# Query rotation without a second projection: DVE reads one PSUM bank with its partition halves exchanged

## The chip, the cores and the metric

The kernel runs on one core of one Trainium2 chip. The metric is the device time of that core for one execution, in microseconds; the kernel before took 1685.34, 1689.40 and 1690.72 us in three runs, median 1689.4. PE is the matrix engine (TensorE), DVE the vector engine (VectorE), ACT the activation engine (ScalarE), POOL is GpSimd, SP the engine that issues DMAs.

## The reference, cut to what matters

The input is 16 sequences of 512 tokens with 128 channels. The program is two layers; each is half a feed-forward step, a mixing step, and another half feed-forward step. Only the first layer's opening stage is touched by the change: layer norm and feed-forward, then layer norm and the query, key and value projections with rotary embedding.

```
s = x @ Win + bin                                # 128 -> 64 channels
h = relu(s[..., None] * W1 + b1)                 # 16 hidden values per channel
x = x + 0.5 * ((h * W2).sum(-1) + b2) @ Wout ...
n = layernorm(x)
q = n @ Wq      # 16 heads of 8
k = n @ Wk      # 4 heads of 8
v = n @ Wv
q = q * cos + rotate_half(q) * sin               # rotate_half: (x1, x2) -> (-x2, x1)
k = k * cos + rotate_half(k) * sin
```

## The kernel before, in words

The stage is `mlp_layer(..., "qkv")`. It works on two sequences (W = 2, called b = 0 and 1) per turn, eight turns' worth of sequences, in a software pipeline: in one turn the code takes the statistics of the newest pair of sequences (`ahead`), transposes and projects the next (`head`), closes the feed-forward step of the one before (`middle`), and makes queries, keys and values of the last (`tail`). Three turns fill the pipeline, the fourth is the first with a `tail`, four turns run in a hardware loop (`Fori`), and three empty it. Each engine runs its own list of instructions in the order in which the code writes them; semaphores join them. All matmuls of this stage have fp32 operands, and each appears in the trace as two records.

The columns of Wq are laid out so that channel p and channel p + 64 (modulo 128) are the two that a rotation joins. Before, PE projects the queries twice: with `wq` (plain) and with `wqs` (columns swapped by half), into two PSUM banks `r_ps[2b]` and `r_ps[2b+1]`. DVE multiplies the first by the cosine table into `a`, the second by the signed sine table into `b` (`rope`, L675), POOL adds `a` and `b` (L614) and then splits the sum in three bf16 parts together with ACT (L547, L551, L620, L626); SP writes the parts to DRAM (L381, L388). Keys go the same way, with 16 channels for each of both sequences in one bank (64 rows used).

The order of the work around the change, on each engine, for one turn in which all four roles are filled:

- PE: 16 matmuls that contract the hidden values (`channels`, L429; for each hidden row j those of sequence 0 and then of sequence 1, each waiting for its `m_hid` tile), transposes for the tail (L282), the output projection (`output`, L442, after ACT has made `m_g_t`, L557), transposes for the head (L282), queries of sequence 0 (L455), the input projection (L487), queries of sequence 1 (L455), keys (L462), values (L469).
- DVE: statistics of the next pair, the residual addition (L686, when PE's L442 is done), statistics of the middle pair, then rotation of queries 0 (L675 twice), five hidden tiles of sequence 0 (`hidden`, L666), rotation of queries 1, five hidden tiles of sequence 1, rotation of the keys, copy of the values (L698).
- ACT: `m_g_t` (L557), copies of transposed tiles, `m_s` (L571, after L487), the other three hidden tiles of each sequence (L575), the normalisations (L219), the parts.
- POOL: L635, parts of the turn before, square roots (L192, L198), then the sums `a + b` (L614).

The query banks are reused in the same turn: keys go to banks 0 and 1 after DVE's reads of queries 0 (`rope_read`), values to bank 2 after DVE's first read of queries 1.

Of the kernel before, what the change touches and what calls it, by code (L numbers as in the profile page):

```python
# [9 lines left out]
ALU = mybir.AluOpType  # L10
# [3 lines left out]
P = 128  # L14
NB = 16
T = 512
D = 128
C = T // P
EPS = 1e-5

NH, NKV = 16, 4
HD = D // NH
# [7 lines left out]
HALF = P // 2  # L30
# [13 lines left out]
W = 2  # L44
# [3 lines left out]

PACK = [("ident", P), ("win2", P), ("bin2", 1), ("w1p", HT), ("b1p", HT), ("w2p", HT), ("b2p", 1), ("wout2", D), ("pairsum", P),
        ("mhalf", W * C), ("wu", M * 4), ("wtop", M), ("maskf", P), ("self", 2 * P), ("gw", E), ("rowbase", 1),  # L50
        ("wq", D), ("wqs", D), ("wk", NKV * HD), ("wks", NKV * HD), ("wv", NKV * HD), ("wo", D)]
PACK_LATE = [("cosq", T), ("sinq", T), ("iota", T)]


# [262 lines left out]
def mlp_layer(nc, sem, h, xres, tail_kind, name, x_in=None, loads=None, v_all=None,  # L317
# [7 lines left out]
    with ExitStack() as tmp:  # L325
# [5 lines left out]
        xhat2_t = [t(f"xhat2_t{b}", [P, T], F32) for b in range(W)]  # L331
# [6 lines left out]
        r_ps = [bank(f"r{j}") for j in range(4)]  # L338
# [30 lines left out]
        with nc.Block() as block:  # L369
# [50 lines left out]
            def _(pe):  # L420
# [13 lines left out]
                def output(i, tail):  # L434

                    pe.wait_ge(g_read, i + 1)
                    for b in range(W):
                        if qkv and tail is not None:

                            after(pe, rope_read, tail * 2 * NT)  # L440
                        for c in range(C):
                            mm = pe.matmul(y_ps[b][:, c * P:(c + 1) * P], g_t[:, c * P:(c + 1) * P], h["woutz"][:, b, :],  # L442
                                           start=True, stop=True)
                        mm.then_inc(y_full, 1)

                def queries(i, b):
                    for j, wt in enumerate(("wq", "wqs")):
                        if b == 1 and j == 0:

                            after(pe, v_read, i)  # L450
                        if b == 0 and j == 0:

                            after(pe, rope_read, i * 2 * NT)
                            pe.wait_ge(x_added, min((i + 2) * W, NB) if isinstance(i, int) else (i + 2) * W)
                        pe.matmul(r_ps[2 * b + j][:], h[wt][:], xhat2_t[b][:], start=True, stop=True).then_inc(rope_full, 1)  # L455

                def keys(i):

                    for j, wt in enumerate(("wk", "wks")):
                        pe.wait_ge(rope_read, i * 2 * NT + j + 1)  # L460
                        for b in range(W):
                            mm = pe.matmul(r_ps[j][b * KR:(b + 1) * KR, :], h[wt][:], xhat2_t[b][:], start=True, stop=True)  # L462
                        mm.then_inc(rope_full, 1)

                def values(i):
                    pe.wait_ge(rope_read, i * 2 * NT + 3)
                    for b in range(W):
                        for c in range(C):
                            mm = pe.matmul(r_ps[2][:, (b * C + c) * KR:(b * C + c + 1) * KR], xhat2_t[b][:, c * P:(c + 1) * P], h["wv"][:],  # L469
                                           start=True, stop=True)  # L470
                    mm.then_inc(v_full, 1)

# [182 lines left out]
            @block.vector  # L655
            def _(dve):
                v = nc.vector

                def hidden(i, *parts):
                    for j in range(made):  # L660
                        for b in parts:
                            dve.wait_ge(s_read, i * W + b + 1)

                            after(dve, hid_used, (i - 1) * HT + j + 1)

                            v.tensor_scalar(hid[b][j][:], s_in[b][:], h["w1p"][:, j:j + 1], h["nb1p"][:, j:j + 1],  # L666
                                            ALU.mult, ALU.max).then_inc(hid_done, 1)

                def rope(i, x):
                    n, rows = TILES[x]  # L670

                    after(dve, parts_out[x], i * OUT[x])
                    for j, (dst, tab) in enumerate((("a", "cos"), ("b", "sin"))):
                        dve.wait_ge(rope_full, (i * NT + x) * 2 + j + 1)
                        v.tensor_tensor(rot[n][dst][:], r_ps[(2 * x + j) % 4][0:rows, :], h[tab + n[0]][:], ALU.mult).then_inc(rope_read, 1)  # L675

                def turn(ahead, head, middle, tail):
                    if ahead is not None:
                        if x_in is not None:
                            dve.wait_ge(x_loaded, ahead + 1)  # L680
                        moments(dve, norm1, ahead)
                    if middle is not None:
                        dve.wait_ge(bias_added, middle + 1)
                        for b in range(W):
                            dve.wait_ge(y_full, middle * W + b + 1)
                            v.tensor_tensor(xres[:, middle * W + b, :], y_ps[b][:], xres[:, middle * W + b, :], ALU.add).then_inc(x_added, 1)  # L686
                        dve.wait_ge(x_added, middle * W + W)
                        moments(dve, norm2, middle)
                    if not qkv and head is not None:
                        hidden(head, *range(W))  # L690
                    for x in range(NT if qkv else 0):
                        if tail is not None:
                            rope(tail, x)
                        if head is not None and x < W:
                            hidden(head, x)
                    if qkv and tail is not None:
                        dve.wait_ge(v_full, tail + 1)
                        v.tensor_copy(v_all[:, bass.ds(tail * W, W), :],  # L698
                                      r_ps[2][:, 0:W * C * KR].rearrange("p (b x) -> p b x", b=W)).then_inc(v_read, 1)
                    if not qkv and tail is not None and not is_first(tail):  # L700
                        gate.keep(dve, tail - 1)
                    if not qkv and ahead is not None:
                        norm1.apply_dve(dve, ahead, xt_full)

                pipeline(dve, turn)
                if not qkv:
                    gate.keep(dve, TURNS - 1)
                    gate.softmax(dve)
# [943 lines left out]
def layouts(i):  # L1652
# [16 lines left out]
        "wq": wq.reshape(D, D), "wqs": wq[:, swap].reshape(D, D), "wk": wk.reshape(D, -1), "wks": wk[:, swap].reshape(D, -1),  # L1669
# [49 lines left out]
```

## Time and profile before

| | |
|---|---|
| three runs | 1685.34, 1689.40, 1690.72 us |
| profiled execution: own time / span | 1689.98 / 1688.3 us |
| stage of the change | from 0 to the first attention matmul at 225.31 us |
| PE busy, whole span | 1445.3 us (86%) |
| DVE / ACT / POOL busy | 1266.1 / 1161.0 / 776.1 us |
| mean granted TensorE clock | 0.925 |

In the rows below, times are microseconds from the span's start. A timeline row merges equal instructions that follow each other: start, length of the whole group, engine, line, operation, output and inputs, shape, count, and in brackets how long the engine was idle before it and what ended that. PE is the matmul, PEld its weight loads. A clock of 1.00 is 2.4 GHz, 0.50 is 1.2 GHz.

### The profile page before, as it was taken

To read this page: it belongs to the slowest core of one execution; us is meant where nothing else is said; L and a number is where in the kernel's file an instruction comes from. 1 tells how busy PE (TensorE), PEld (TensorE's weight loads), DVE (VectorE), ACT (ScalarE), POOL (GpSimd) and SP (SyncE) were. 2 spreads that over 40 slices of the span, in tenths; PEclk is the share of its full clock that TensorE was granted. 3 is DMA by queue.
4 is the path that set the end of the run, shared out by engine and by line. 5 is a ranking of instruction groups with operands and counts; after the bars stand their busy time and mean duration, and the time that the engine had idled before them with its cause. 6 is when DMAs were issued, how large, how long until landed. Compare 5 with 4: busy or idle time off the path is not lost. (4 is left out here: it accounts for less than half of the span.)

```text
span 1688.3 us, 40713 instructions
## 1 busy us (share of the span) xinstructions
PE 1445.3 (86%) x12722; PEld 1002.4 (59%) x12722; DVE 1266.1 (75%) x3158; ACT 1161.0 (69%) x2439; POOL 776.1 (46%) x1204
## 2 busy tenths in 40 slices
PE   3899859999999999969980899999968708999998
PEld 1455434545445454425550799999835508999997
DVE  3677568888888888737848577877788585778776
ACT  3788527777777777757862688778656507787875
POOL 2578734545454444424424666554022106665540
PEclk9999959999999999979985899999978758999999
DMA  5022211111111111000112111111001101111110
GB/s 153 10 70 84 88 31 41 45 39 46 41 44 46 39 44 41 10 1 26 37 38 100 37 38 38 33 30 26 1 13 44 44 0 40 51 51 50 48 36 25
DMA packets 84640, 70.92 MB, mean 42 GB/s; under 512 B 16752, under 2 KB 78000, under 8 KB 84528
## 3 DMA queue, kind: packets, MB, share of 16 engines
q1 hardware_dynamic: 76336, 52.62, 11.2%
q0 software_dynamic: 8192, 16.79, 3.9%
q8 instruction: 72, 1.18, 0.3%
q14 instruction: 40, 0.33, 0.1%
HBM read 46.81 MB, written 22.54 MB: 41 GB/s over the span
## 5 line engine op out<-in xcount | busy, mean ns | idle before, releaser
L1081 DVE TENSOR_REDUCE at_negmax<-at_s_ps 128x2 f32<-128x1024 f32 (+3 forms) x384 | 389.4, 1044 | 65.0 <-PE at_s_ps L858 57.6
L987 ACT ACTIVATE at_p<-at_x_ps 128x512 f32<-128x512 f32 x640 | 355.2, 596 | 97.3 <-PE at_x_ps L870 90.6
L1301 POOL DMA_INDIRECT e_x_in<-xn,e_row_c x256 | 258.9, 1011 | 145.8 <-issue 79.6
L1042 POOL TENSOR_SCALAR_AFFINE_SELECT at_p<-at_p 128x256 f32<-128x256 f32 (+1 forms) x448 | 190.4, 439 | 242.5 <-ACT at_p L987 242.4
L870 PE MATMUL at_x_ps<-qr,kr 50*128 50x512 bf16 (+3 forms) x1024 | 226.8, 304 | 18.7 <-ACT at_p L987 11.0
L1422 DVE TENSOR_TENSOR e_hid_lo<-e_hid,e_hid_hi 128x512 fp32r<-128x512 f32 x256 | 177.2, 692 | 83.0 <-ACT e_hid_hi L1386 70.3
L853 PE MATMUL at_s_ps<-kr,qr 48*128 48x512 bf16 (+3 forms) x1024 | 188.1, 311 | 19.2 <-PEq L1636 12.8
L1385 ACT ACTIVATE e_hid<-e_h_ps 128x512 f32<-128x512 f32 x256 | 154.8, 605 | 41.3 <-PE e_h_ps L1327 36.5
L886 PE MATMUL at_o_ps<-at_p,at_va 128*32 128x512 f32 (+3 forms) x2048 | 178.8, 445 | 0.0
L870 PEld LDWEIGHTS at_x_ps<-qr,kr 50*128 50x128 bf16 x1024 | 66.4, 94 | 153.0 <-ACT at_p L987 137.7
L1327 PE MATMUL e_h_ps<-e_x_hi,w_hi 128*128 128x256 f32 x512 | 156.7, 306 | 0.0
L858 PE MATMUL at_s_ps<-maskb,selb 64*128 64x64 bf16 x2048 | 156.3, 193 | 0.0
L1386 ACT ACTIVATE e_hid_hi<-e_h_ps 128x512 fp32r<-128x512 f32 x256 | 155.7, 608 | 0.0
L1327 PE MATMUL e_h_ps<-e_x_hi,w_lo 128*128 128x256 f32 x512 | 146.0, 285 | 0.0
L1327 PE MATMUL e_h_ps<-e_x_lo,w_hi 128*128 128x256 f32 x512 | 145.6, 284 | 0.0
L1337 PE MATMUL e_yt_ps<-e_hid_hi,w_lo 128*128 128x256 f32 x512 | 144.3, 282 | 0.0
L1337 PE MATMUL e_yt_ps<-e_hid_hi,w_hi 128*128 128x256 f32 x512 | 144.1, 281 | 0.0
L1337 PE MATMUL e_yt_ps<-e_hid_lo,w_hi 128*128 128x256 f32 x512 | 144.0, 281 | 0.0
L858 PEld LDWEIGHTS at_s_ps<-maskb,selb 64*128 64x128 bf16 x2048 | 124.7, 98 | 31.7 <-issue 3.4
L1378 ACT ACTIVATE e_x_hi<-e_t_ps 128x256 fp32r<-128x256 f32 x128 | 49.5, 386 | 135.5 <-PE e_t_ps L1316 124.3
L1355 PE MATMUL e_acc_ps<-e_hot,e_y_hi 128*128 128x512 f32 x256 | 111.6, 436 | 3.0 <-DVE e_hot L1441 3.0
L1441 DVE TENSOR_SCALAR e_hot<-pack_late,e_loc_c 128x512 fp32r<-128x512 f32 x256 | 114.1, 488 | 0.0
(196 smaller groups left out, 3391.2 us busy)
## 6 DMA issues: line engine op xcount, KB each, us to landing
qr<-q_parts SPq DMA_DIRECT2D x128, 48.0 KB
kr<-k_parts SPq DMA_DIRECT2D x128, 48.0 KB
xres<-in_x_dram SPq DMA_DIRECT2D x8, 512.0 KB, 7.4
qr<-q_parts SPq DMA_DIRECT2D x128, 32.0 KB
xn<-m_n_xhat SPq DMA_DIRECT2D x16, 256.0 KB
e_x_in<-xn,e_row_c POOLq DMA_INDIRECT x256
xn<-sc_n_xhat SPq DMA_DIRECT2D x16, 256.0 KB
out_dram<-xres SPq DMA_DIRECT2D x16, 256.0 KB
```

The source lines that it names most:

```text
L853: pe.matmul(s_ps[k % 2][:, half * T + a * w:half * T + (a + 1) * w], qr[u][rows, q0:q0 + P], kr[u][rows, g * T:g * T + w], start=True, sto ...
L858: mm = pe.matmul(s_ps[k % 2][:, at:at + HALF], h["selb"][rows, x * P:(x + 1) * P], h["maskb"][rows, x * HALF:(x + 1) * HALF], start=False, ...
L870: mm = pe.matmul(x_ps[i % 2][:, at:at + T - c * P], kr[u][rows, g * T + c * P:g * T + (c + 1) * P], qr[u][rows, q0 + c * P:q0 + T], start= ...
L886: mm = pe.matmul(o_ps[32 * j:32 * j + 32, c * P:T], va[u][:, c, g, :], p_sb[g % 2][:, i, at:at + T - c * P], start=(c == 0 and g % 2 == 0) ...
L987: a.activation(p_sb[g % 2][:, i, :], x_ps[i % 2][:], ACT.Exp, scale=SCALE).then_inc(x_read, 1)
L1042: sel = gp.affine_select(out=part, in_=part, compare_op=ALU.is_ge, fill=0.0, base=0, pattern=[[0, n] for n in part.shape[1:-1]] + [[1, P]] ...
L1081: v.tensor_reduce(out, scored, AX.X, ALU.max, negate=True).then_inc(s_read, 1)
L1301: nc.gpsimd.indirect_dma_start(out=x_in[k][u][:], out_offset=None, in_=xn_dram, in_offset=bass.IndirectOffsetOnAxis(ap=row_c[k][:, u:u + 1 ...
L1327: mm = pe.matmul(h_ps[half][:, f, :], w1[:, k, at:at + P], x[k % 2][:], start=(j == 0), stop=(j == len(pairs) - 1))
L1337: mm = pe.matmul(yt_ps[:], w2[:, k, f * D:(f + 1) * D], x[k % 2][:, f, :], start=(f == 0 and j == 0), stop=(f == FC - 1 and j == len(pairs ...
L1386: a.activation(hid_hi[k % 2][:, half * HC:(half + 1) * HC, :], h_ps[half][:], ACT.Gelu).then_inc(gelu_done, 1)
L1422: v.tensor_tensor(hid_lo[k % 2][:, chunks, :], hid[half][:], whole(hid_hi[k % 2][:, chunks, :]), ALU.subtract).then_inc(hl_done, 1)
```

## The change

The weights `wqs` are gone from the packed constants (128 columns less in the one DMA that loads them), and with them one of the two query matmuls of each sequence, 16 in all. DVE's cosine product is as before. The sine product becomes two instructions of 64 partitions each: the lower half of `b` from the upper half of the bank, the upper half of `b` from the lower half. `rope_read` still rises twice per query tile, the second time at the last of the three.

The banks are dealt out anew: queries 0 in bank 0, queries 1 in bank 2, keys in banks 1 and 3 (which no query uses now, so the wait ahead of the keys goes), values in bank 0 once DVE has read queries 0 whole. Two waits for `v_read` move with the values' bank.

```
-        ("wq", D), ("wqs", D), ("wk", NKV * HD), ...
+        ("wq", D), ("wk", NKV * HD), ...
 def queries(i, b):
-    for j, wt in enumerate(("wq", "wqs")):
-        if b == 1 and j == 0:
-            after(pe, v_read, i)
-        if b == 0 and j == 0:
-            after(pe, rope_read, i * 2 * NT)
-            pe.wait_ge(x_added, ...)
-        pe.matmul(r_ps[2 * b + j][:], h[wt][:], xhat2_t[b][:], ...).then_inc(rope_full, 1)
+    if b == 0:
+        after(pe, rope_read, i * 2 * NT)
+        after(pe, v_read, i)
+        pe.wait_ge(x_added, ...)
+    pe.matmul(r_ps[2 * b][:], h["wq"][:], xhat2_t[b][:], ...).then_inc(rope_full, 2)
 def keys(i):
-        pe.wait_ge(rope_read, i * 2 * NT + j + 1)
...
-            mm = pe.matmul(r_ps[j][b * KR:(b + 1) * KR, :], ...)
+            mm = pe.matmul(r_ps[2 * j + 1][b * KR:(b + 1) * KR, :], ...)
 def values(i):
-    pe.wait_ge(rope_read, i * 2 * NT + 3)
+    pe.wait_ge(rope_read, i * 2 * NT + 2)
...
 def rope(i, x):
-    for j, (dst, tab) in enumerate((("a", "cos"), ("b", "sin"))):
-        dve.wait_ge(rope_full, (i * NT + x) * 2 + j + 1)
-        v.tensor_tensor(rot[n][dst][:], r_ps[(2 * x + j) % 4][0:rows, :], h[tab + n[0]][:], ALU.mult).then_inc(rope_read, 1)
+    if x < W:
+        full = r_ps[2 * x]
+        dve.wait_ge(rope_full, (i * NT + x) * 2 + 2)
+        v.tensor_tensor(r["a"][:], full[:], h["cosq"][:], ALU.mult).then_inc(rope_read, 1)
+        v.tensor_tensor(r["b"][0:HALF, :], full[HALF:P, :], h["sinq"][0:HALF, :], ALU.mult)
+        v.tensor_tensor(r["b"][HALF:P, :], full[0:HALF, :], h["sinq"][HALF:P, :], ALU.mult).then_inc(rope_read, 1)
```

On PE, in the first turn that has a tail, the rows before are these: transposes, two matmuls of queries 0, two of the input projection, two of queries 1, four of keys, eight of values.

```order
L282 MATMUL m_xt_ps<-pack,m_n_xhat 128x128 x8
L455 MATMUL m_r_ps<-m_xhat_t,pack 128x512 x2
L487 MATMUL m_s_ps<-m_xhat_t,pack 128x512 x2
L455 MATMUL m_r_ps<-m_xhat_t,pack 128x512 x2
L462 MATMUL m_r_ps<-m_xhat_t,pack 32x512 x4
L469 MATMUL m_r_ps<-pack,m_xhat_t 128x32 x8
```

The same place on PE in the changed kernel, whose lines are numbered a little lower:

```order
L282 MATMUL m_xt_ps<-pack,m_n_xhat 128x128 x8
L453 MATMUL m_r_ps<-m_xhat_t,pack 128x512
L484 MATMUL m_s_ps<-m_xhat_t,pack 128x512 x2
L453 MATMUL m_r_ps<-m_xhat_t,pack 128x512
L459 MATMUL m_r_ps<-m_xhat_t,pack 32x512 x4
L466 MATMUL m_r_ps<-pack,m_xhat_t 128x32 x8
```

One matmul ahead of the input projection and one behind it are gone; nothing else has moved.

On DVE, the same turn before and after, from the rotation of queries 0 to the copy of the values:

```order
 L675 TENSOR_TENSOR m_q0a<-m_r_ps,pack_late 128x512
-L675 TENSOR_TENSOR m_q0b<-m_r_ps,pack_late 128x512
-L666 TENSOR_SCALAR m_hid<-m_s,pack,nb1p 128x512 x5
+L676 TENSOR_TENSOR m_q0b<-m_r_ps,pack_late 64x512
+L677 TENSOR_TENSOR m_q0b<-m_r_ps,pack_late 64x512
+L663 TENSOR_SCALAR m_hid<-m_s,pack,nb1p 128x512 x5
 L675 TENSOR_TENSOR m_q1a<-m_r_ps,pack_late 128x512
-L675 TENSOR_TENSOR m_q1b<-m_r_ps,pack_late 128x512
-L666 TENSOR_SCALAR m_hid<-m_s,pack,nb1p 128x512 x5
```

Each query tile has three products instead of two, and both stand ahead of the hidden tiles of sequence 1 (the second L666 group).

## Rows read from the trace of the kernel before

**Rows 1.** Busy time by stretch: PE, PEld, DVE, ACT, POOL, clock, DMA, GB/s.

```profile
103.00:124.00 21.00, 20.12 (x102) 10.56 (x101) 16.79 (x55) 17.57 (x36) 17.28 (x16) 1.00 0.30 84
```

**Rows 2.** Timeline of PE, one turn of the loop.

```profile
146.64 2.05 PE L442 MATMUL m_r_ps<-woutz,m_g_t 128*128 128x128 f32 x16 [0.79 <-ACT m_g_t L557]
149.67 1.96 PE L455 MATMUL m_r_ps<-m_xhat_t,pack 128*128 128x512 f32 x4
151.47 1.88 PE L487 MATMUL m_s_ps<-m_xhat_t,pack 128*128 128x512 f32 x4
156.83 1.97 PE L469 MATMUL m_r_ps<-pack,m_xhat_t 128*128 128x32 f32 x16
158.73 7.11 PE L429 MATMUL m_xt_ps<-m_hid,w2d 128*64 128x512 f32 x32
165.78 1.09 PE L282 MATMUL m_s_ps<-pack,m_n_xhat 128*128 128x128 f32 x8
```

**Rows 3.** Timeline of ACT, the same turn.

```profile
145.84 0.67 ACT L557 ACTIVATE m_g_t<-m_xt_ps,gbias 128x512 f32<-128x512 f32 x1
152.52 0.69 ACT L571 ACTIVATE m_s<-m_s_ps,pack 128x512 f32<-128x512 f32 x1 [1.77 <-PE m_s_ps L487]
166.86 0.66 ACT L557 ACTIVATE m_g_t<-m_xt_ps,gbias 128x512 f32<-128x512 f32 x1
```

**Rows 4.** Timeline of DVE, the same turn, from several narrow windows.

```profile
148.84 0.69 DVE L686 TENSOR_TENSOR xres<-m_r_ps,xres 128x512 f32 x1 [0.20 <-PE m_r_ps L442]
...
153.12 0.68 DVE L675 TENSOR_TENSOR m_q0b<-m_r_ps,pack_late 128x512 f32<-128x512 f32 x1
153.71 2.36 DVE L666 TENSOR_SCALAR m_hid<-m_s,pack,nb1p 128x512 f32<-128x512 f32 x5
...
157.19 0.96 DVE L666 TENSOR_SCALAR m_hid<-m_s,pack,nb1p 128x512 f32<-128x512 f32 x1
...
158.07 1.95 DVE L666 TENSOR_SCALAR m_hid<-m_s,pack,nb1p 128x512 f32<-128x512 f32 x2
```

**Rows 5.** Timeline of PE's weight loads, an earlier turn of the loop.

```profile
96.58 0.19 PEld L429 LDWEIGHTS m_xt_ps<-m_hid,w2d 128*64 128x64 f32 x3 [0.29 <-DVE m_hid L666]
```

**Rows 6.** Groups of instructions, 0 to 235 us: busy us, mean ns, idle before.

```profile
L675 DVE TENSOR_TENSOR m_ka<-m_r_ps,cosk 64x512 f32<-64x512 f32 x8 | 5.4, 676 | 1.9 <-DMA k_parts<-m_kparts 1.9
```

**Rows 7.** Timeline of DVE at the program's start: half-tile copies.

```profile
15.55 0.22 DVE L117 COPY woutz<-pack 64x128 f32<-64x128 f32 x1
15.79 0.23 DVE L118 TENSOR_SCALAR yrow<-yrow 128x128 f32<-128x128 f32 x1
```

**Rows 8.** Timeline of POOL, the same turn as rows 2.

```profile
156.60 1.27 POOL L614 TENSOR_TENSOR m_q0a<-m_q0a,m_q0b 128x512 f32<-128x512 f32 x1
157.83 1.45 POOL L614 TENSOR_TENSOR m_q1a<-m_q1a,m_q1b 128x512 f32<-128x512 f32 x1
```

**Rows 9.** Timeline of DVE, the first turn with queries.

```profile
68.96 1.96 DVE L666 TENSOR_SCALAR m_hid<-m_s,pack,nb1p 128x512 f32<-128x512 f32 x2
```

**Rows 10.** Timeline of PE, the first turn with queries, and one turn ahead of it.

```profile
52.56 7.08 PE L429 MATMUL m_xt_ps<-m_hid,w2d 128*64 128x512 f32 x30 [1.21 <-DVE m_hid L666]
...
72.03 1.97 PE L469 MATMUL m_r_ps<-pack,m_xhat_t 128*128 128x32 f32 x16 [0.97 <-DVE m_q1a L675]
73.93 8.78 PE L429 MATMUL m_xt_ps<-m_hid,w2d 128*64 128x512 f32 x32
```

**Rows 11.** Busy time by stretch, as rows 1: the channels of rows 10.

```profile
74.16:77.57 3.41, 3.41 (x10) 0.98 (x8) 3.41 (x9) 2.58 (x7) 1.36 (x2) 0.50 0.00 0
```

**Rows 12.** Timelines of PE and DVE, the first turn that empties the pipeline.

```profile
187.35 1.09 PE L282 MATMUL m_s_ps<-pack,m_n_xhat 128*128 128x128 f32 x8
...
178.89 2.40 DVE L666 TENSOR_SCALAR m_hid<-m_s,pack,nb1p 128x512 f32<-128x512 f32 x3
```

**Rows 13.** Timelines of DVE and POOL, the end of the stage.

```profile
207.21 0.69 DVE L675 TENSOR_TENSOR m_q0a<-m_r_ps,pack_late 128x512 f32<-128x512 f32 x1 [8.20 <-DMA q_parts<-m_q0parts]
208.68 1.27 POOL L614 TENSOR_TENSOR m_q0a<-m_q0a,m_q0b 128x512 f32<-128x512 f32 x1 [0.66 <-DVE m_q0b L675]
```

More of the change, by code:

```diff
@@ L50 @@
         ("mhalf", W * C), ("wu", M * 4), ("wtop", M), ("maskf", P), ("self", 2 * P), ("gw", E), ("rowbase", 1),
-        ("wq", D), ("wqs", D), ("wk", NKV * HD), ("wks", NKV * HD), ("wv", NKV * HD), ("wo", D)]
+        ("wq", D), ("wk", NKV * HD), ("wks", NKV * HD), ("wv", NKV * HD), ("wo", D)]
 PACK_LATE = [("cosq", T), ("sinq", T), ("iota", T)]
@@ L440, in output @@
                             after(pe, rope_read, tail * 2 * NT)
+                            after(pe, v_read, tail)
                         for c in range(C):
@@ L446, in queries @@
                 def queries(i, b):
-                    for j, wt in enumerate(("wq", "wqs")):
-                        if b == 1 and j == 0:
-                            after(pe, v_read, i)
-                        if b == 0 and j == 0:
-                            after(pe, rope_read, i * 2 * NT)
-                            pe.wait_ge(x_added, min((i + 2) * W, NB) if isinstance(i, int) else (i + 2) * W)
-                        pe.matmul(r_ps[2 * b + j][:], h[wt][:], xhat2_t[b][:], start=True, stop=True).then_inc(rope_full, 1)
+                    if b == 0:
+                        after(pe, rope_read, i * 2 * NT)
+                        after(pe, v_read, i)
+                        pe.wait_ge(x_added, min((i + 2) * W, NB) if isinstance(i, int) else (i + 2) * W)
+                    pe.matmul(r_ps[2 * b][:], h["wq"][:], xhat2_t[b][:], start=True, stop=True).then_inc(rope_full, 2)
                 def keys(i):
                     for j, wt in enumerate(("wk", "wks")):
-                        pe.wait_ge(rope_read, i * 2 * NT + j + 1)
                         for b in range(W):
-                            mm = pe.matmul(r_ps[j][b * KR:(b + 1) * KR, :], h[wt][:], xhat2_t[b][:], start=True, stop=True)
+                            mm = pe.matmul(r_ps[2 * j + 1][b * KR:(b + 1) * KR, :], h[wt][:], xhat2_t[b][:], start=True, stop=True)
                         mm.then_inc(rope_full, 1)
                 def values(i):
-                    pe.wait_ge(rope_read, i * 2 * NT + 3)
+                    pe.wait_ge(rope_read, i * 2 * NT + 2)
                     for b in range(W):
                         for c in range(C):
-                            mm = pe.matmul(r_ps[2][:, (b * C + c) * KR:(b * C + c + 1) * KR], xhat2_t[b][:, c * P:(c + 1) * P], h["wv"][:],
+                            mm = pe.matmul(r_ps[0][:, (b * C + c) * KR:(b * C + c + 1) * KR], xhat2_t[b][:, c * P:(c + 1) * P], h["wv"][:],
                                            start=True, stop=True)
@@ L672, in rope @@
                     after(dve, parts_out[x], i * OUT[x])
-                    for j, (dst, tab) in enumerate((("a", "cos"), ("b", "sin"))):
-                        dve.wait_ge(rope_full, (i * NT + x) * 2 + j + 1)
-                        v.tensor_tensor(rot[n][dst][:], r_ps[(2 * x + j) % 4][0:rows, :], h[tab + n[0]][:], ALU.mult).then_inc(rope_read, 1)
+                    r = rot[n]
+                    if x < W:
[4 more added lines that the diff above has]
+                        v.tensor_tensor(r["b"][HALF:P, :], full[0:HALF, :], h["sinq"][HALF:P, :], ALU.mult).then_inc(rope_read, 1)
+                    else:
+                        for j, (dst, tab) in enumerate((("a", "cosk"), ("b", "sink"))):
+                            dve.wait_ge(rope_full, (i * NT + x) * 2 + j + 1)
+                            v.tensor_tensor(r[dst][:], r_ps[2 * j + 1][0:rows, :], h[tab][:], ALU.mult).then_inc(rope_read, 1)
                 def turn(ahead, head, middle, tail):
@@ L698, in turn @@
                         v.tensor_copy(v_all[:, bass.ds(tail * W, W), :],
-                                      r_ps[2][:, 0:W * C * KR].rearrange("p (b x) -> p b x", b=W)).then_inc(v_read, 1)
+                                      r_ps[0][:, 0:W * C * KR].rearrange("p (b x) -> p b x", b=W)).then_inc(v_read, 1)
                     if not qkv and tail is not None and not is_first(tail):
@@ L1668, in layouts @@
         "wout2": twice(a["L0_ffn_Wout"]), "bout": a["L0_ffn_bout"][None, :],
-        "wq": wq.reshape(D, D), "wqs": wq[:, swap].reshape(D, D), "wk": wk.reshape(D, -1), "wks": wk[:, swap].reshape(D, -1),
+        "wq": wq.reshape(D, D), "wk": wk.reshape(D, -1), "wks": wk[:, swap].reshape(D, -1),
         "wv": a["L0_attn_Wv"], "wo": a["L0_attn_Wo"],
```

## The prediction, made before the changed kernel was run

> **What bounds the kernel now.** I read the page first, then busy time by stretch, then the four engines' timelines over one and the same turn, and last the waits. The page shows PE as the busiest engine over the whole span, but only the first 225 of 1688 us hold the change, so everything is read there. A turn of the loop is 21.0 us, and PE is busy for 20.12 of it [rows 1]: by that row alone PE looks like the bound, and any matmul taken away should be time. The timelines say it less simply. PE does have one gap in each turn, 0.79 us ahead of L442, and ACT ends it [rows 2]. ACT's own turn runs from one `m_g_t` at 145.84 to the next at 166.86, 21.02 us [rows 3], and hangs on PE at one point: `m_s` at 152.52 waits for L487. So the loop that sets the pace is `m_g_t`, L442, transposes, queries 0, input projection, `m_s`, ACT's list, `m_g_t`.
>
> There is a second loop close beside it, through DVE. L442 ends, DVE adds (148.84), takes statistics, rotates queries 0 (the sine product at 153.12), makes hidden tiles 0 (153.71), rotates queries 1, makes hidden tiles 1 from 157.19 [rows 4], and PE's L429 needs these in turn: for each hidden row first sequence 0, then sequence 1. The second tile of sequence 1 is ready at 158.07 + 1.95 minus one plain tile (0.54, less its 0.08 of overlap), near 159.57. That is when PE, which starts L429 at 158.73 and does two matmuls in 0.88 us, wants it. The weight load of an earlier turn in fact waits for `m_hid` there [rows 5]. From L429's end (L282 at 165.78 [rows 2]) ACT could start `m_g_t` some 0.1 us later, at 165.9, and starts at 166.86. So the DVE loop has about 0.95 us to spare in a turn, and the PE loop about as much.
>
> **The change part by part.**
>
> PE, removed: 2 matmuls per turn. The four records of one query pair last from 149.67 to 151.47, 1.80 us for two matmuls [rows 2], so 0.90 each; 16 make 14.4 us of PE time. One of a turn's two is in ACT's loop (ahead of L487): that loop falls from 21.02 to 20.1. The other only lets PE reach the values and L429 earlier, by 1.8 us in all.
>
> PE, waits: the keys' wait goes; the values now need queries 0 read whole. DVE finishes that near 153.71 + 0.9 = 154.6 of this turn; PE would reach the values at 156.83 - 1.80 = 155.0. No stall, but only 0.4 us of cover. The added wait for `v_read` of the turn before has long been met. Behind the values stands L429, so PE comes to it at 156.9 and finds hidden tiles 1 missing.
>
> DVE, added: the sine product is two instructions of 64 partitions. The trace has 64-partition products, on the keys: 676 ns each [rows 6], the same as the 0.68 us of 128 partitions [rows 4], so halving the partitions saves nothing. In a row of plain products one starts 0.60 us after the other (153.12 to 153.71 [rows 4]). That is the lower bound: +0.60 per tile. The upper bound comes from the start of the program, where a copy into the upper half of a tile stands: it starts at 15.55 and takes 0.22, and the full-tile instruction behind it starts at 15.79 [rows 7]. Where partitions change, neighbours don't overlap; elsewhere in this stage they overlap by 0.08 to 0.09. Three such borders per tile (into the exchanged half, into the other half, out to the hidden tile) cost 3 x 0.094 = 0.28. I take +0.88 per tile, 1.76 per turn, since these rows have the same form of change; the lower bound is 1.20.
> The Trainium skill, VectorE: DVE Perf Modes, section "Two Vector instructions with no wait between them", says that an instruction whose first input or output starts in another group of 32 partitions than the one before starts only when every earlier Vector instruction has finished. The trace agrees (15.55 + 0.22 against 15.79). By the rule a turn costs 1.76 us of DVE, without it 1.20; nothing else in the sum rests on it.
>
> The loop turn. Hidden tiles 1 start at 157.19 + 1.76 = 158.95. POOL then matters. A hidden tile that starts while POOL runs L614 takes far longer: five plain ones take 2.36 [rows 4], so one 0.54 and two 1.00 with their overlap, and two take 1.96 when the second meets L614 [rows 9]: 0.96 for one meeting. Before, both L614 (156.60 and 157.83 [rows 8]) fall on the first two hidden tiles 1. Now the first L614 runs beside the rotation, and the second follows the rotation, so one tile is free and the second meets it: it is ready 1.95 after the start (as in the first turn), at 160.9, which is 1.33 later than 159.57. L282 therefore comes at 165.78 + 1.35 = 167.13, `m_g_t` at 167.24, and the turn lasts 21.4 instead of 21.02. **+0.38 for each of 4 loop turns, +1.5.** With 1.20 in place of 1.76 it is 20.85, a gain of 0.16 per turn. PE idles near 1.8 us in it, between its first L429 matmul and the next.
>
> POOL and hidden tiles 0. They now start at 154.6 and the last of five at 156.42. The L614 of queries 0 starts at 156.60, and perhaps 0.1 to 0.3 earlier since POOL's square root meets fewer hidden tiles. If it comes first, one hidden tile 0 is held up too, 0.96 per turn [rows 9]. Bounds 0 and 4 x 0.96 = 3.8; the row is within 0.2 of the border, so I take half, **+1.9**.
>
> The first turn with queries. DVE's hidden tiles 1 come 1.76 later there too, but PE is already slowed: L429 took 8.78 instead of 7.11 [rows 2, 10]. It starts its second matmul near 74.9 and ends about 0.5 later. **+0.5**.
>
> The first emptying turn. L282 follows L429 at 187.35, and the second hidden tile 1 is ready at 178.89 + 1.95 = 180.84 [rows 12], so PE didn't wait. Plus 1.76 it is 182.6, and the seven remaining steps need 6.15 (7.01 for all eight, by the 7.08 at 52.56, which has the same start [rows 10]): L282 at 188.85. **+1.5**; with the lower DVE cost +0.9.
>
> The end of the stage is POOL's chain. DVE starts the last queries 0 at 207.21 when a DMA has landed, POOL adds at 208.68 [rows 13], and works on nearly without a gap until the key parts go out and the stage ends. No PE work is in this chain, so the removed matmuls are worth nothing here, and the third product is in it whole: **+0.8** (0.60 to 0.88).
>
> The constants: 64 KB less in a load that the whole start waits for, at the page's 153 GB/s of the first slice: 0 to -0.4, **-0.3**.
>
> The clock. In 74.16:77.57 the granted clock was 0.50, that is 1.2 GHz [rows 11], right after PE had waited 0.97 us and done 16 short records of the values [rows 10]; L429 then cost 1.67 us more. After 1.21 us of waiting amid long matmuls (52.56) it stayed at 1.00, as L429's 7.08 shows. The changed turn has 1.9 us of values, one L429 matmul, then 1.8 us of idling: more like the first. Over five turns (loop and first emptying) the cost is between 0 and 5 x 1.67 = 8.4. Part of a slow stretch would fall on the idling itself, and where it falls drifts from turn to turn, so I take three times 0.85, **+2.5**.
>
> Sum: 1.5 + 1.9 + 0.5 + 1.5 + 0.8 - 0.3 + 2.5 = +8.4 against the profiled execution's own 1689.98, so 1698.4. The median of the runs is 0.6 lower than that execution, which gives 1697.8, said as 1698.
>
> **The rivals.**
>
> A, the DVE work is hidden. If borders cost nothing, POOL doesn't meet hidden tiles 0 and the clock holds: 4 x -0.16 + 0.9 + 0.6 - 0.3 + 0.1 = +0.7, 1690. For it: 0.95 us per turn of cover on DVE's loop. Against: the copies at 15.55 [rows 7], and all three must hold at once.
>
> B, the matmuls are the bound after all. ACT's loop gives 4 x -0.92 = -3.7, the other turns with PE near full up to -1.8: 1684. For it: PE's 20.12 of 21.0 and ACT's loop [rows 3]. Against: it needs DVE's tiles to come no later than now, and the trace shows them just in time already [rows 4, 5].
>
> C, the clock decides: if each of five turns falls to 0.50 for its L429 and both hidden groups meet L614, the sum is 1.5 + 3.8 + 0.5 + 1.5 + 0.8 + 8.4 = +16.5, 1706. It decides if the gap of every turn does what the gap of the first turn with queries did [rows 10]. For it: the new gap is twice the 0.97 there. Against: the stretch drifts, and 1.21 did not do it.
>
> **How the numbers follow.** A measurement of this kernel tells 0.3% (5.1 us) from no change. My forecast 0.62 (1693 to 1703), A 0.20, B 0.10, C 0.08. Slower by over 0.3% (above 1694.5) takes C and most of the forecast's case: 0.66. Faster by over 0.3% (below 1684.3) takes half of B and a little for what I have missed: 0.08. Within: 0.26. The range goes from A's lower side to just short of C: 1688.5 to 1705.
>
> **What would show it.** In the profile after: PE's L453 at 32 records; L429 in loop turns with a wait on `m_hid` after its first matmul, 1.5 to 3 us; no bracket "ACT m_g_t" ahead of L443; turns of 21.4 to 23.5 us; L676 and L677 starting 0.69 apart; a hidden tile of about 1.5 us in both groups or only in the second; clock 0.50 in some L429; POOL's L614 of the last pair starting 2.3 us after DVE's q0a, where it is 1.47 now. It is wrong if turns are shorter than 21.0, if L429 runs without a wait, or if the halves overlap.

## The result, and the profile after

The changed kernel took 1708.38 us (median of four runs, 1707.06 to 1709.97) where the kernel before took 1689.82 (also four). The ratio is 1.0116, with a 95% interval of 1.0103 to 1.0129: slower by 18.6 us, where 8.4 had been predicted. The time lies above the predicted range; its direction was right, its size was not.

The profiled execution has an own time of 1709.14 us, a span of 1707.4 and a mean clock of 0.918. The starts of the eight output projections (L442 before, L443 after) and of the first attention matmul show where the time went in:

| | before | after | added |
|---|---|---|---|
| second projection | 60.90 | 61.74 | +0.84 |
| third (first turn with queries) | 83.58 | 85.47 | +1.05 |
| fourth to seventh (four loop turns) | 167.58 | 180.74 | +11.27 |
| eighth (first emptying turn) | 188.28 | 204.43 | +2.99 |
| first attention matmul | 225.31 | 242.13 | +0.67 |
| last attention output | 735.1 | 754.0 | +2.1 |

Each loop turn grew by 2.75 to 2.91 us. The last column is what each interval added by itself, not the running total. Timeline of PE after, one loop turn (compare [rows 2]):

```profile
109.25 2.02 PE L443 MATMUL m_r_ps<-woutz,m_g_t 128*128 128x128 f32 x16
...
114.90 1.02 PE L453 MATMUL m_r_ps<-m_xhat_t,pack 128*128 128x512 f32 x2
115.86 1.91 PE L459 MATMUL m_r_ps<-m_xhat_t,pack 128*32 128x512 f32 x8
117.69 1.97 PE L466 MATMUL m_r_ps<-pack,m_xhat_t 128*128 128x32 f32 x16
119.60 1.07 PE L429 MATMUL m_xt_ps<-m_hid,w2d 128*64 128x512 f32 x2
123.21 8.89 PE L429 MATMUL m_xt_ps<-m_hid,w2d 128*64 128x512 f32 x30 [2.54 <-DVE m_hid L663]
132.04 1.09 PE L282 MATMUL m_s_ps<-pack,m_n_xhat 128*128 128x128 f32 x8
133.07 1.13 PE L443 MATMUL m_r_ps<-woutz,m_g_t 128*128 128x128 f32 x8
```

Two things stand out. PE runs through to its first L429 matmul and then stands for 2.54 us until DVE has the first hidden tile 1 (1.8 had been predicted). The other L429 matmuls then take 8.89 us instead of some 7.1. No bracket names `m_g_t` ahead of L443: the PE/ACT loop of [rows 3] no longer sets the pace.

DVE in the same turn (compare [rows 4]):

```profile
115.09 0.69 DVE L675 TENSOR_TENSOR m_q0a<-m_r_ps,pack_late 128x512 f32<-128x512 f32 x1
115.81 0.69 DVE L676 TENSOR_TENSOR m_q0b<-m_r_ps,pack_late 64x512 f32<-64x512 f32 x1
116.52 0.68 DVE L677 TENSOR_TENSOR m_q0b<-m_r_ps,pack_late 64x512 f32<-64x512 f32 x1
117.23 3.33 DVE L663 TENSOR_SCALAR m_hid<-m_s,pack,nb1p 128x512 f32<-128x512 f32 x5
120.48 0.68 DVE L675 TENSOR_TENSOR m_q1a<-m_r_ps,pack_late 128x512 f32<-128x512 f32 x1
...
122.61 4.16 DVE L663 TENSOR_SCALAR m_hid<-m_s,pack,nb1p 128x512 f32<-128x512 f32 x5
...
130.78 3.37 DVE L186 TENSOR_SCALAR m_n_less<-m_n_mv 128x8 f32<-128x8 f32 x1 [0.16 <-DVE m_n_mv L179]
```

The products start 0.71 to 0.72 apart, and so does the hidden tile behind them, instead of 0.60: the borders cost 0.11 each, as forecast (0.094). Both hidden groups are long. POOL, same turn (compare [rows 8]), tells why:

```profile
118.72 1.56 POOL L611 TENSOR_TENSOR m_q0a<-m_q0a,m_q0b 128x512 f32<-128x512 f32 x1
122.76 1.53 POOL L611 TENSOR_TENSOR m_q1a<-m_q1a,m_q1b 128x512 f32<-128x512 f32 x1 [2.48 <-DVE m_q1b L677]
124.24 1.34 POOL L617 TENSOR_TENSOR m_q0b<-m_q0a,m_q0parts 128x512 f32<-128x512 f32 x1
...
130.50 1.16 POOL L623 TENSOR_TENSOR m_q0parts<-m_q0b,m_q0parts 128x512 bf16<-128x512 f32 x1
131.62 2.50 POOL L632 TENSOR_TENSOR xres<-xres,yrow 128x512 f32 x2
```

The last hidden tile 0 is on DVE when L611 runs at 118.72, and among hidden tiles 1 the second meets L611 and the third meets L617. Of the five single records in that second group, 0.55, 1.49, 1.37, 0.54 and 0.53 us long, the two long ones are these. The statistics instruction L186, 8 elements wide, takes 3.37 us while POOL works through three instructions without a gap (L623 and the two L632); before, it took 0.62 to 0.65 in the loop.

The clock, by stretch, in three loop turns of the changed kernel (compare [rows 11]; the columns are those of [rows 1]):

```profile
123.80:127.20 3.40, 3.40 (x10) 0.96 (x8) 3.40 (x5) 2.21 (x5) 1.78 (x2) 0.50 0.22 57
147.70:151.10 3.40, 3.40 (x10) 0.97 (x9) 3.40 (x5) 2.28 (x5) 1.72 (x2) 0.50 0.14 36
171.60:175.00 3.40, 3.40 (x12) 0.73 (x10) 3.40 (x5) 2.27 (x5) 1.73 (x2) 0.50 0.06 19
```

The granted clock is 0.50 (1.2 GHz) just behind the gap in every turn: at 76.0, 99.9, 123.8, 147.7, 171.6 and 195.5, each 23.9 us after the one before, about as long as the turn itself (23.75 to 23.91). Before, this part of the stage had one such stretch, at 74.1.

### The profile page after: what moved, and what is told of

The parts are those of the page before. It is cut to its first block and busy times, and to the rows that moved or that the text cites. A ratio compares the mean times of both kernels' runs of the same rounds, so it can differ in the third digit from the quotient of the medians.

```text
span 1707.4 us, 40666 instructions
## 1 busy us (share of the span) xinstructions
PE 1450.5 (85%) x12690; PEld 1001.0 (59%) x12690; DVE 1298.5 (76%) x3174; ACT 1162.2 (68%) x2439; POOL 777.1 (46%) x1204
## 5 line engine op out<-in xcount | busy, mean ns | idle before, releaser
L1391 ACT ACTIVATE e_hid<-e_h_ps 128x512 f32<-128x512 f32 x256 | 155.1, 606 | 43.2 <-PE e_h_ps L1333 37.9
```

## The experiments

Ratios are medians against the kernel before, run beside it, with 95% intervals. Code is cut to the lines that matter, and rows to those that the reading needs. "Turn" is the distance between output projections in the loop.

**1. PE's relief alone: one full sine product, no third product, no exchange.**

```
-v.tensor_tensor(r["b"][0:HALF, :], full[HALF:P, :], h["sinq"][0:HALF, :], ALU.mult)
-v.tensor_tensor(r["b"][HALF:P, :], full[0:HALF, :], h["sinq"][HALF:P, :], ALU.mult).then_inc(rope_read, 1)
+v.tensor_tensor(r["b"][:], full[:], h["sinq"][:], ALU.mult).then_inc(rope_read, 1)
```

> The changed kernel with the sine product as one instruction of 128 partitions that reads the bank straight. Left out: the exchange of the halves. So PE loses its 16 matmuls and DVE gains nothing. In the changed kernel a loop turn lasts 23.85 us, in the kernel before 21.0. Theory (the added DVE work is the whole loss, by way of late hidden tiles, POOL and the clock): turns of 20.1 us, set by ACT's loop; L429 at 7.1 us; about 1685.5 us, ratio 0.997. Rival 1 (any shortening of PE's list makes PE idle and lowers the clock): L429 at 8.8 us in each turn, turns near 21.8, 1693 us or more. Rival 2 (the re-dealt banks and moved waits cost time by themselves): over 1695 us at full clock.

Measured: 1684.16, ratio 0.9964 [0.995, 0.9977]; loop turns of 20.25 at clock 1.00. The missing matmuls do bring time, 0.77 us per turn, and the newly dealt banks cost none. So the loss comes with the third product and the borders on DVE, and with what follows from them.

**2. The third product, but no borders** (three plain 128-partition products).

```
+v.tensor_tensor(spare[x][:], full[:], h["sinq"][:], ALU.mult)
+v.tensor_tensor(r["b"][:], full[:], h["sinq"][:], ALU.mult).then_inc(rope_read, 1)
```

> The changed kernel with three sine and cosine products of 128 partitions, all from partition 0, the additional one into a tile that nobody reads. Left out: the exchange. DVE gains 16 instructions but no border between partition groups. Theory (0.60 us per instruction, and 0.28 per tile for borders, which push the hidden tiles of sequence 0 into POOL's L611): products start 0.60 apart, hidden tiles 0 take 2.36 again, turns between 20.9 us (clock 1.00) and 22.6 (clock falls in L429): 1690 to 1698 us. Rival (the count of DVE instructions is all, borders don't matter): turns of 23.8 and 1707 us as in the changed kernel.

Measured: 1701.40, ratio 1.0076 [1.0045, 1.0106], above the theory's range and below the rival's. DVE, a group from a short turn of the loop and then a long turn:

```profile
92.77 2.36 DVE L664 TENSOR_SCALAR m_hid<-m_s,pack,nb1p 128x512 f32<-128x512 f32 x5
...
105.52 4.05 DVE L186 TENSOR_SCALAR m_n_less<-m_n_mv 128x8 f32<-128x8 f32 x1 [0.16 <-DVE m_n_mv L179]
...
113.82 0.69 DVE L676 TENSOR_TENSOR m_q0a<-m_r_ps,pack_late 128x512 f32<-128x512 f32 x1
114.42 0.68 DVE L677 TENSOR_TENSOR m_spare<-m_r_ps,pack_late 128x512 f32<-128x512 f32 x1
115.02 0.68 DVE L678 TENSOR_TENSOR m_q0b<-m_r_ps,pack_late 128x512 f32<-128x512 f32 x1
115.62 3.32 DVE L664 TENSOR_SCALAR m_hid<-m_s,pack,nb1p 128x512 f32<-128x512 f32 x5
...
120.66 4.20 DVE L664 TENSOR_SCALAR m_hid<-m_s,pack,nb1p 128x512 f32<-128x512 f32 x5
```

The products are 0.60 apart, so the borders are gone. The loop's turns are 20.9, 26.1, 20.9 and 24.7 us, of two kinds. In the short ones hidden tiles 0 go free (2.36), as expected, and only hidden tiles 1 meet POOL (4.25). In the long ones both groups meet it (3.32 and 4.20), L429 (L430 here) falls into a slow stretch (9.95 us for 30 records in the turn shown), and PE waited 2.05 us for DVE's residual addition, which stood behind an L186 of 4.05 us: a second hold-up that the prediction did not have. Without borders the kernel is 7 us faster than the changed one; since the parts don't add up (experiment 5), that is not a price of the borders in themselves.

**3. Keep PE busy in the gap** with three spare matmuls ahead of L429.

```
+def filler(head):
+    pe.wait_ge(s_read, head * W + W)
+    for _ in range(3):
+        pe.matmul(s_ps[0][:], h["wq"][:], xhat2_t[0][:], start=True, stop=True)
```

> The changed kernel, and PE does three spare 128x512 matmuls into a free bank at the end of each turn, where it would idle 2.5 us for the hidden tiles. Theory (the idling costs the clock in each turn, 1.75 us of L429): clock 1.00 in L429, its 30 records take 7.1 instead of 8.8, turns of 22.1 us, 1699.5 us. Rival 1 (late DVE tiles decide alone, the slower L429 is hidden): 1708 us as now. Rival 2 (the spare matmuls delay L429 itself): over 1709 us.

Measured: 1703.51, ratio 1.0074 [1.0047, 1.0101]. No L429 of the loop fell into a slow stretch (7.1 us for 32 records where DVE was in time); two such stretches lay elsewhere in its turns (89.3 and 116.6). Yet turns were 23.2 to 25.7 us, where the theory had 22.1. DVE, then PE, in a turn of 25.66:

```profile
108.79 4.05 DVE L186 TENSOR_SCALAR m_n_less<-m_n_mv 128x8 f32<-128x8 f32 x1 [0.16 <-DVE m_n_mv L179]
...
113.86 1.27 DVE L699 TENSOR_TENSOR xres<-m_r_ps,xres 128x512 f32 x2
```

```profile
109.39 2.02 PE L443 MATMUL m_r_ps<-woutz,m_g_t 128*128 128x128 f32 x16
...
115.28 1.10 PE L453 MATMUL m_r_ps<-m_xhat_t,pack 128*128 128x512 f32 x2 [3.00 <-DVE xres L699]
```

The L186 hold-up is in the changed kernel too, but there the slow L429 covers it (experiment 7). Once L429 is fast it comes to light: PE has L443's result at 111.4 and the addition starts 2.5 us later.

**4. Take away the meetings**: POOL's sum on 16 of 512 columns.

```
-g.tensor_tensor(r["a"][:], r["a"][:], r["b"][:], ALU.add)
+g.tensor_tensor(r["a"][:, 0:16], r["a"][:, 0:16], r["b"][:, 0:16], ALU.add)
```

> The changed kernel, with POOL's sums a + b (L611) on 16 of 512 columns. Left out: most of the addition. Theory (each full L611 that meets a hidden tile costs 0.96 us): both groups of hidden tiles take 2.4 us unless L617 meets the second, turns of 20.9 us at clock 1.00 or 22.6 with a fall; the end of the stage 3 us shorter; 1692 to 1700 us. Rival (hidden tiles are slow for another reason, such as the SBUF reads of SP's DMAs, or L611 is not the partner): hidden groups of 3.3 and 4.2 us remain, turns near 23.8, only the end of the stage gains, 1704 us.

Measured: 1690.06, ratio 1.0018 [1.0003, 1.0032]. DVE and then PE, in the one turn of its loop that had a slow clock:

```profile
112.48 2.37 DVE L663 TENSOR_SCALAR m_hid<-m_s,pack,nb1p 128x512 f32<-128x512 f32 x5
...
116.91 2.37 DVE L663 TENSOR_SCALAR m_hid<-m_s,pack,nb1p 128x512 f32<-128x512 f32 x5
```

```profile
104.49 2.02 PE L443 MATMUL m_r_ps<-woutz,m_g_t 128*128 128x128 f32 x16
...
117.50 8.78 PE L429 MATMUL m_xt_ps<-m_hid,w2d 128*64 128x512 f32 x30 [1.59 <-DVE m_hid L663]
...
127.25 1.02 PE L443 MATMUL m_r_ps<-woutz,m_g_t 128*128 128x128 f32 x7
```

With the half-tile products and all their borders in place, turns are 21.06, as long as before the change, and 22.76 in this one. Next to the changed kernel's 23.8 the difference is two groups of hidden tiles at 2.37, and a clock that falls once and not every time. This time is below the theory's 1692 to 1700. The short sum also relieves POOL itself (from the eighth projection to the first attention matmul it is 35.1 us, in the changed kernel 37.7), so this run takes more away than the meetings alone.

**5. The other way round: the kernel before, with a third product.**

```
+if x < W and j == 1:
+    v.tensor_tensor(spare[x][:], r_ps[(2 * x + j) % 4][0:rows, :], h[tab + n[0]][:], ALU.mult)
```

> The kernel before, both query matmuls kept, with a third product of 128 partitions per query tile on DVE, into a tile that nobody reads: the added DVE work without the removed PE work. Theory (DVE's lateness costs because PE, now 1.8 us early, idles beside the short matmuls of the values and loses the clock): with PE on time L429 keeps 7.1 us, turns stay at 21.0 to 21.3, ratio 1.000 to 1.002. Rival (the count of DVE instructions decides whatever PE does): as with the three plain products on the changed kernel, turns of 21 to 26 us, ratio near 1.0076.

Measured: 1693.05, ratio 1.0023 [1.0011, 1.0034]; turns of 21.03 as before. The two halves of the change don't add up: fewer matmuls alone -0.36%, a plain third product alone +0.23%, the two together (experiment 2) +0.76%. What the third product costs here lies outside the loop: 2.2 us in the first emptying turn, where both groups meet POOL, and 1.2 ahead of the second projection, at a slow stretch (52.5) that may not be its doing. DVE and POOL show one reason why the loop stays free:

```profile
114.05 2.36 DVE L667 TENSOR_SCALAR m_hid<-m_s,pack,nb1p 128x512 f32<-128x512 f32 x5
...
118.12 3.33 DVE L667 TENSOR_SCALAR m_hid<-m_s,pack,nb1p 128x512 f32<-128x512 f32 x5
```

```profile
115.98 1.57 POOL L615 TENSOR_TENSOR m_q0a<-m_q0a,m_q0b 128x512 f32<-128x512 f32 x1
118.39 1.41 POOL L615 TENSOR_TENSOR m_q1a<-m_q1a,m_q1b 128x512 f32<-128x512 f32 x1 [0.83 <-DVE m_q1b L678]
```

The fifth hidden tile 0 starts at 115.87, a tenth of a microsecond ahead of L615, and is let through at 0.54; hidden tiles 1 meet one instruction. So it is in experiment 2's short turns; in its long turns, behind the long L186, the sum (L612) came at 116.18, between the starts of the second and third hidden tile.

**6 and 7. Take away what holds up L186**: L632 on 4 columns per group instead of 128, with the spare matmuls of experiment 3 (6) and without (7).

```
-bias = g.tensor_tensor(x, x, h["yrow"][:].unsqueeze(1).to_broadcast([P, C, D]), ALU.add)
+bias = g.tensor_tensor(x[:, :, 0:4], x[:, :, 0:4], h["yrow"][:, 0:4].unsqueeze(1).to_broadcast([P, C, 4]), ALU.add)
```

> The changed kernel with the three spare matmuls (1703.5 us), and POOL adds its output bias (L632) on 16 of 512 columns. Left out: most of that addition. In the run with spare matmuls DVE's tiny L186 took over 3 us while POOL ran L623 and L632, and PE then waited 2.6 to 3.0 us for the residual addition. Theory (POOL holds up L186, which gave back what the clock brought): L186 below 1.5 us, no wait of PE ahead of L453, turns of 22 to 22.7, 1693 to 1698 us. Rival (PE's wait comes from elsewhere, the spare matmuls' own wait or ACT): turns near 24.5 remain, over 1701 us.

> The changed kernel, and only POOL's bias addition (L632) on 16 of 512 columns; the spare matmuls are not there. Left out: most of that addition. Theory (in the changed kernel the slow L429 hides L186's 3.4 us, so L186 costs nothing there): L186 short, turns still 23.5 to 23.9 with clock 0.50 in L429, 1706 to 1708.5 us. Rival (L186 costs time in the changed kernel too): 1698 us or less with the clock still low.

Measured: 1700.04, ratio 1.0068 [1.0046, 1.009], and 1705.90, ratio 1.0102 [1.008, 1.0123]. In both L186 fell to 0.89. With the spare matmuls the turns became an even 23.0, and PE no longer waited for the residual addition; the hold-up of experiment 3 is thereby shown, though the time stayed above the 1693 to 1698 expected. Without them turns stayed at 23.7 to 23.9, clock 0.50 in each: in the changed kernel itself L186 is hidden. Three turns of experiment 6 at full clock, with PE busy for 67.53 of 69.04 us, its spare matmuls counted in:

```profile
84.02:153.06 69.04, 67.53 (x306) 33.81 (x307) 60.43 (x171) 53.33 (x106) 46.12 (x45) 1.00 0.23 69
```

**8. PE as full as before, by the same matmul done twice**, DVE as in the changed kernel.

```
+pe.matmul(r_ps[2 * b][:], h["wq"][:], xhat2_t[b][:], start=True, stop=True)
 pe.matmul(r_ps[2 * b][:], h["wq"][:], xhat2_t[b][:], start=True, stop=True).then_inc(rope_full, 2)
```

> The changed kernel with the plain query matmul done twice into the same bank, so that PE has as many 512-column matmuls ahead of L429 as before, while DVE keeps the half-tile products with their borders. Theory (the length of the turn comes from DVE's later hidden tiles plus a clock that falls because PE idles beside short matmuls; PE full ahead of L429 keeps the clock and moves the meeting with POOL): turns of 21.4 to 22.6 us, granted clock 1.00 in L429 of nearly every turn, a wait on m_hid of 0.5 to 1.6 us, ratio 1.002 to 1.007. Rival 1 (the borders themselves and both meetings with POOL set the turn whatever PE does): turns of 22.9 to 23.9 us, ratio 1.009 to 1.013. Rival 2 (DVE's work is all hidden once PE is full): turns of 21.0, ratio 1.000 to 1.002.

Measured: 1705.24, ratio 1.0107 [1.0089, 1.0126]: by its time the first rival, not my theory, and not clearly less than the changed kernel's 1.0116 [1.0103, 1.0129]. The six runs went from 1700.07 to 1710.63, and the profiled one, with 1700.48, is at their low end, so its turns are better than the usual ones. PE in a loop turn:

```profile
107.68 2.02 PE L443 MATMUL m_r_ps<-woutz,m_g_t 128*128 128x128 f32 x16
...
119.74 1.07 PE L429 MATMUL m_xt_ps<-m_hid,w2d 128*64 128x512 f32 x2
121.65 1.16 PE L429 MATMUL m_xt_ps<-m_hid,w2d 128*64 128x512 f32 x4 [0.83 <-DVE m_hid L664]
123.06 6.26 PE L429 MATMUL m_xt_ps<-m_hid,w2d 128*64 128x512 f32 x26 [0.25 <-DVE m_hid L664]
...
130.28 1.91 PE L443 MATMUL m_r_ps<-woutz,m_g_t 128*128 128x128 f32 x15
```

The clock is 1.00 here and the turn still 22.60 (another is 22.52). DVE's hidden tiles 1 start at 121.05, 13.37 after L443; in the changed kernel they start at 122.61, 13.36 after L443. From there to the next L443 it is 9.23 here and 10.46 there. So this run splits the changed turn: 22.6 is DVE's path with its meetings, and 1.23 is the clock. The other two turns of this loop show both further costs: a slow clock in L429 (23.72), and an L186 of 4.47 us with a 1.92 us wait of PE behind it and then a slow stretch in the queries and the input projection (24.78). PE as full as before does not by itself keep the clock.

**9. Change DVE's order**: both hidden groups directly behind the rotation of queries 0; ACT's normalisation ahead of its splits.

```
-                        if head is not None and x < W:
-                            hidden(head, x)
+                        if head is not None and x == 0:
+                            hidden(head, 0)
+                            hidden(head, 1)
```

> The changed kernel with DVE's list of a turn in another order: rotation of queries 0, hidden tiles 0, hidden tiles 1, then the rotation of queries 1 and of the keys; ACT applies the first norm of the turn ahead before it splits the early tiles. The output is complete. Theory (the turn is long because hidden tiles 1 stand behind the second rotation on DVE): hidden tiles 1 start some 2.4 us earlier, L429 runs without a wait and at full clock, turns of 20.9 to 21.4 us, ratio 0.999 to 1.003. Rival (the later rotation of queries 1 and keys delays POOL's and ACT's list by as much, and these set the turn): turns above 22 us, ratio 1.005 to 1.012.

Measured: 1691.89, ratio 1.0027 [1.0017, 1.0037]. DVE:

```profile
112.04 5.60 DVE L663 TENSOR_SCALAR m_hid<-m_s,pack,nb1p 128x512 f32<-128x512 f32 x10
117.57 0.68 DVE L675 TENSOR_TENSOR m_q1a<-m_r_ps,pack_late 128x512 f32<-128x512 f32 x1
```

Ten hidden tiles in 5.60 us, where the changed kernel takes 3.33 + 4.16. The total is in the theory's range. The turns are uneven, though: 20.26 at best, 22.2 to 23.8 where L429 falls into a slow stretch or PE waits for the late rotation of queries 1 (1.37 us ahead of the values), so "without a wait and at full clock" did not hold.

**10 and 11. Exchange the halves by DMA**: one full sine product into a tile `turned`, SP moves its halves crosswise into `b`, POOL subtracts. In 10 for every turn, in 11 only for the first six, the two last turns with the half-tile products.

```
+                            sp.dma_start(rot[f"q{b}"]["b"][dst * HALF:(dst + 1) * HALF, :],
+                                         turned[b][src * HALF:(src + 1) * HALF, :]).then_inc(swapped[b], 16)
...
+                        v.tensor_tensor(turned[x][:], full[:], h["sinq"][:], ALU.mult).then_inc(rope_read, 1)
```

> A complete version: one query matmul, two DVE products of 128 partitions (the sine product into a tile of its own), and SP exchanges its halves by two DMAs of 128 KB; POOL subtracts instead of adding, since the signed sine differs between the halves in sign alone. DVE's list is as long as before, PE's shorter by 16 matmuls. Theory: turns between those of the two-product run (20.25) and 20.9, where POOL waits for a landing; the end of the stage some 2 us later per DMA in its chain, 1685 to 1690 us. Rival (the landing, some 2 us after each product, lands in POOL's and so in ACT's loop): turns of 21.5 and more, over 1692 us.

> The version in which one 128-partition sine product goes to a spare tile and two DMAs exchange its halves, now only for the first six query turns; the last two, while the stage empties, use the half-tile products straight from the bank. The output is complete. Theory (loop turns gain from the matmul taken away when DVE has no added product; the exchange costs only where the stage empties, since its DMA latency lies on POOL's chain there): turns of 20.7 us in the loop, and from the first emptying turn to the first attention matmul 37.5 to 39.5 us, where the version with the exchange everywhere took 42.5 and the kernel before 37.0; ratio 0.996 to 0.998. Rival (the 42.5 came from elsewhere, or the direct products cost as much there): ratio 0.999 to 1.001.

Measured: 1687.93, ratio 0.9996 [0.9986, 1.0006], and 1687.84, ratio 0.9994 [0.9985, 1.0003]. Both show loop turns of 20.75, and both are as fast as the kernel before within the measurement, not faster. PE in a turn of 10:

```profile
122.79 2.02 PE L456 MATMUL m_r_ps<-woutz,m_g_t 128*128 128x128 f32 x16 [1.28 <-ACT m_g_t L567]
...
133.14 8.09 PE L442 MATMUL m_xt_ps<-m_hid,w2d 128*64 128x512 f32 x32
```

From the eighth projection to the first attention matmul version 10 took 42.5 us, the kernel before 37.0, and version 11 took 37.7: a DMA inside POOL's chain costs where no other work covers it. Version 11 reached attention at 221.7, 3.6 us ahead of the kernel before. Its median kept less than half of that; in its profile attention began with a longer slow stretch (below), and the expected 0.996 to 0.998 was missed.

## Why the prediction failed

**What bounds the kernel** was read rightly: PE's and DVE's loops close beside each other, and experiments 1 and 5 show both.

**The borders** (term of 3 x 0.094 per tile): 0.11 each. From the sine product's start to the hidden tile it was 0.59 in [rows 4] and is 1.42, and the cosine product ahead takes 0.11 more: 0.94 per tile, where 0.88 was forecast.

**The loop turn, +0.38.** Its step "one tile is free and the second meets it" was half right. The second does, and a third meets L617, which stands next in POOL's list and which I had not looked up. The group lasts 4.16, and PE waits a second time (0.25 in experiment 8).

**POOL and hidden tiles 0: the step that failed first.** I put L611 within 0.2 us of the last tile and took half of the 3.8. Counted from the output projection, the last tile starts where forecast (9.81 us behind it, at 119.06; 9.78 forecast), but L611 comes 9.47 behind it, at 118.72, where it had been 9.96 before and 0.1 to 0.3 sooner had been allowed. So POOL was first, and the group lasts 3.33 us in each of the six turns that have it: the whole 0.96 per turn, not half. Half stood for not knowing which came first. It isn't a rule that such a meeting comes in all turns or none: in experiment 2 it came in two of four. DVE's path gives turns of 22.6, +1.58 over 21.02, against 0.38 + 0.48 predicted.

**The clock, +2.5: the step that was mis-sized most.** "Where it falls drifts from turn to turn" was wrong. The slow stretches came once per turn, just behind the gap. By experiment 8 the clock is worth 1.23 us of a turn, some 6 us over five turns (an estimate from one turn), not 2.5. Experiments 6 and 7 differ by 0.8 per turn, with the spare matmuls in PE's list. 1.23 is below the 1.67 of rival C, since part of the slow stretch runs while PE would have waited anyway: in experiment 8 those 30 records of L429 take 7.67 us with their waits, not 7.1. The cause of the lock isn't settled. The gap was 2.46 to 2.73 us in each of the six turns, and in experiment 7 too; with gaps of 1.59 in experiment 4 and 0.83 in experiment 8 the clock fell in some turns and not in others, and in the kernel before (74.1) and in experiment 5 (76.4 and 182.2) it fell where L429 had no wait within it.

**First query turn**: +1.05 for 0.5. **First emptying turn**: +2.99 for 1.5 plus a fifth of the clock's term, again both meetings and a slow stretch at 195.5. **End of stage**: +0.67 for 0.8, and L611 starts 2.29 us after DVE's `m_q0a` (223.36 to 225.65), as said. **Constants**: no gain to be seen; the start of the first projection varies between 43.2 and 44.3 over all these kernels.

**What was not in the sum.** A slow stretch at 52.1, ahead of the first queries, stands behind the +0.84 at the second projection; it occurs in experiments 2 to 5 and 11 and not in 1 and 6 to 10, changed turn or not, so I don't count it as an effect of the change. And attention took 2.1 us longer: the slow clock with which it begins ended 29.8 us after its first matmul before, and 35.3 us after it in the changed kernel.

```profile
229.70:277.50 47.80, 29.32 (x292) 14.57 (x292) 29.05 (x30) 13.68 (x27) 15.72 (x33) 0.50 0.11 33
277.50:290.00 12.50, 10.94 (x160) 5.30 (x154) 9.19 (x10) 9.71 (x19) 6.38 (x18) 1.00 0.13 31
```

In the five profiles where that stretch ended 34 to 36 us in (the changed kernel, experiments 5, 6, 7 and 11), attention lasted 510.9 to 511.8; in the other eight, where it ended 28 to 31 us in, 508.9 to 509.9. That goes together in 13 profiles; no run changes the one without the other. If it is the cause, a gain or loss of 2 us in an earlier stage can be doubled or wiped out there.

**Rival C** was priced at 16.5 and given 0.08: both meetings and a clock fall per turn. Both meetings and a clock fall came in each of the six turns, and the loss was 18.6. Against it I had set that the slow stretch drifts and that a gap of 1.21 did not lower the clock; the first was wrong, the second says nothing of a gap of 2.5. That its 16.5 is so near the 16.8 which the stage lost is partly luck: its clock (8.4) was too dear, and it had neither L617 nor the stretch at 52.1.

## What to carry to other kernels

When two loops stand within a microsecond of each other, price an edit that relieves one and loads the other by the second loop alone, with all its neighbours. List every instruction of the engine that shares a resource, not just the first, and where two starts lie within 0.3 us of each other, give the time for both orders, each with a chance, in place of their mean. Where a gap opens ahead of a long run of matmuls, count a slow clock for each turn, and test the count with spare work in the gap before believing it.

## What the runs showed of the hardware

A DVE `tensor_scalar` of 128x512 fp32 takes 0.54 us alone and 1.37 to 1.52 when a POOL `tensor_tensor` has begun up to 0.35 us before it. An 8-element one takes 0.17 alone and up to 4.47 when POOL has several instructions in a row. The rotation's products, which read one operand from PSUM, stayed at 0.67 to 0.69 beside the same POOL work (0.68 at 156.59 in the kernel before, with L614 from 156.60). The Trainium skill, SBUF — State Buffer, section "Who interferes with whom", says that a Vector instruction in a two-port mode and a GpSimd instruction exclude each other, and that whoever comes first keeps the ports for its whole length. The traces agree as to the tile that starts 0.1 us ahead of POOL's sum and goes free (experiment 5). When a waiting DVE instruction is let in between POOL instructions that follow each other without a gap is not settled. In the changed kernel L186, at 130.78, was held through L623 and both L632 and ended with the last of them, after 3.37 us; in experiment 3 one of 4.05 us ended at 112.84, while POOL went straight on. In the kernel before it started beside the first of two L635 and ended at 147.53, with that one (1.28 us from 146.23), though the second followed without a gap:

```profile
146.23 2.52 POOL L635 TENSOR_TENSOR xres<-xres,yrow 128x512 f32 x2 [0.58 <-ACT m_n_xhat L219]
146.91 0.62 DVE L186 TENSOR_SCALAR m_n_less<-m_n_mv 128x8 f32<-128x8 f32 x1 [0.16 <-DVE m_n_mv L179]
```

Two engines changed one at a time gave -0.36% and +0.23%, and +0.76% together; with the exchange of halves it was +1.16%.
